# Routing of four mixture-of-experts stages: six slot one-hots on ScalarE, a residual shift moved behind the tiles, two of four weight guesses issued with the rows

## The chip, the cores and the metric

One core of one Trainium2 chip runs one program. The metric is the device time of one execution in microseconds, taken as the median over runs. Engines by their names in the profile: PE (TensorE), DVE (VectorE), ACT (ScalarE), POOL (GpSimd), SP (Sync, which here only issues DMAs); PEld is TensorE's weight load.

## The reference

Four layers over x of 1024 nodes x 256 features. Each layer adds a graph attention (or graph convolution) of the normalised x, and then a mixture of experts of the normalised x in which every row goes to its top two experts. The part that the change touches is the mixture, here that of layer 0, the residual form with a layer norm behind it:

```python
gate_logits = x @ gate_w + gate_b
topk_vals, topk_idx = jax.lax.top_k(gate_logits, K)            # K = 2
topk_w = jax.nn.softmax(topk_vals, axis=-1)
h = jax.nn.relu(jnp.einsum('bsh,ehf->bsef', x, w1) + b1)
expert_out = jnp.einsum('bsef,efh->bseh', h, w2) + b2
...
y = x + moe
return (y - mu) / jnp.sqrt(var + EPS) * gamma + beta
```

Layers 0 and 3 have 16 experts, layers 1 and 2 have 8; hidden widths are 512, 512, 1024 and 512 (layer 3 with two up projections and silu). Layer 2 adds one shared expert that every row passes through.

## The kernel before

The program runs four graph stages and four expert stages in turn, on all five engines, ordered by semaphores that are written out by hand; each engine executes its own queue in order. I call the expert stages 0 to 3 after their layers.

**Routing (`gate`).** An expert stage sorts its 2048 (row, expert) pairs into tiles of 128 rows of one expert. DVE makes one-hots of the chosen experts, TensorE counts ranks, and DVE derives for each pair a slot in its tile (`slot_f`, signalled by `slots_known`) and a tile (`on_tile`). The table of which row stands in which slot is a sum of 16 matmuls (`tensor_table`, L1490): the left factor is `on_slot`, 16 one-hots of 128x128, the right one `token`. Before the change GpSimd makes the first four `on_slot` one-hots (`pool_part`, L1509) and DVE the other twelve in one instruction (L1565); ScalarE makes one column of `token` (`scalar_column`, L1503, then a warm-up call of the stage's function, L1504). TensorE waits for all three, and then keeps itself busy with 56 matmuls of no result (`rouse`). `vector_rows` turns the sum into row numbers (`rows_known`, L1579), `first_rows` copies the first indices (L2008), and `vector_experts` writes the expert of each tile to `etab` (`tiles_known`, L1584).

**Expert tiles (`experts`).** Stages 0, 1 and 3 have UN = 4 buffers, stage 2 has 2. Per tile: GpSimd gathers 128 rows from DRAM with an indirect DMA (L1858, software queue q0), TensorE transposes them (`turn`, L1882), DVE copies them (L2004), TensorE multiplies by w1 (`rise`, L1894), ScalarE activates, and TensorE multiplies by w2 (`fall`, L1909) with operands that ScalarE and DVE split in two. Stage 2 first runs eight `own` tiles of the shared expert, with the routing between them.

**Weights (Sync queue, q1).** Before the routing is known, Sync loads a guessed expert into each of the UN buffers: two DMAs per buffer (L1810, L1811), about 1.05 MB together in stages 0 and 1, 1.57 MB in stage 3. Then it issues the load of the second biases (`biases.load`) and `after.prefetch`: in stage 0 five loads for the next graph stage, among them `gamma` and `beta`. Then it waits for `tiles_known`, and per tile reads the true expert and issues the DMA under the condition that the expert is another than the one guessed or held (L1829, L1834). A skipped DMA still counts up its semaphore, which `rise` waits for. In the timeline a skipped one of these shows about 0.01 to 0.1 us, an issued one 0.3 and more.

**The end of stage 0 (`BeforeGraph1`).** Its second half also works out the layer norm of the mixture with gamma and beta. `vector_early` runs on DVE ahead of the first tile: it prepares `a_parted` and a column of V, waits for gamma and beta, and adds beta to all of x (L1047). After the tiles TensorE sums the second biases, DVE adds them (L1651), the sums are loaded and normalised; GpSimd's powers (L972, L976) give the reciprocal deviations.

Of the kernel before, what the change touches and what calls it, by code (L numbers as in the profile page):

```python
# [15 lines left out]
P = 128  # L16
N = 1024
NT = N // P
# [8 lines left out]
def build(nc, A, out):  # L27
# [19 lines left out]
    with top:  # L47
# [27 lines left out]
        iota_p, spent = keep("iota_p", [P, 1]), keep("spent", [P, 1])  # L75
# [233 lines left out]
        class LastLayer:  # L309
# [25 lines left out]
            def vector_early(self, dve):  # L335
                pass
# [14 lines left out]
        class Handover:  # L351
# [3 lines left out]
            def vector_early(self, dve):  # L355
                pass
# [32 lines left out]
        def constants_vector(dve, link, iota_i, iota_pi, lane_i, turn_i, made, roused):  # L389
            nc.vector.memset(ones_b[:, :], 1.0).then_inc(roused, 1)  # L390
            nc.vector.memset(table[:, :], 0)
            nc.vector.memset(power[:, :, :], -0.5).then_inc(roused, 1)
            nc.vector.memset(xn[:, :, D:D + 1], 1.0)
            dve.wait_ge(made, 2)
            nc.vector.tensor_copy(iota_p[:, :], iota_pi[:, :])
            for un in (UN_NARROW, UN_WIDE):
                nc.vector.tensor_scalar(lane_i[un][:, :], iota_i[:, 0:32], un - 1, None, ALU.bitwise_and)
                nc.vector.tensor_scalar(turn_i[un][:, :], iota_i[:, 0:32], un.bit_length() - 1, None,
                                        ALU.logical_shift_right)
            link(nc.vector.tensor_copy(iota_row[:, :], iota_i[:, :]))  # L400
            nc.vector.tensor_scalar(code_row[:, :, :], bc(iota_row[:, 0:2 * NT].unsqueeze(2), [P, 2 * NT, 32]),
                                    float(CODE), None, ALU.add)
            link(nc.vector.tensor_scalar(own[:, :], iota_row[:, 0:32], float(P), float(OWN + CODE * P), ALU.mult, ALU.add))
            nc.vector.tensor_scalar(own[:, :], own[:, :], iota_p[:, :], None, ALU.add)
            for un in (UN_NARROW, UN_WIDE):
                nc.vector.tensor_copy(lane_rows[un][:, :], lane_i[un][:, :])
                nc.vector.tensor_copy(turn_rows[un][:, :], turn_i[un][:, :])
                nc.vector.tensor_scalar(part_rows[un][:, :], iota_row[:, 0:32], 1.0 / un, None, ALU.mult)
                nc.vector.tensor_scalar(iota_uns[un][:, :], iota_row[:, 0:32], float(un), None, ALU.mult)
# [515 lines left out]
        class BeforeGraph1(Handover):  # L925
# [4 lines left out]
            def __init__(self, ph):  # L930
                H, DH = self.H, self.DH
                self.rest = ph.sb("rest", [P, NT, H])
                self.dst = ph.sb("dst", [P, H, N])
                self.V = ph.sb("V", [P, NT, H, DH + 1])
                self.w = ph.sb("w", [P, DC, D])
                self.wr = ph.sb("wr", [P, DC, D])
                self.a = ph.sb("a", [P, DC, 2])
                self.a_parted, self.parted = ph.sb("a_parted", [P, DC, 2, 2]), ph.sem("parted")
                self.wa = ph.sb("wa", [P, DC, H])
                self.wab = ph.sb("wab", [P, DC, H, P])  # L940
                self.weights_loaded, self.post_loaded = ph.sem("weights_loaded"), ph.sem("post_loaded")
                self.folded, self.spread = ph.sem("folded"), ph.sem("spread")
                self.columns, self.valued = ph.sem("columns"), ph.sem("valued")
                self.columns_kept, self.values_kept = ph.sem("columns_kept"), ph.sem("values_kept")
# [23 lines left out]
            def gpsimd(self, pool):  # L968
                for t in range(NT + 1):
                    if t < NT:  # L970
                        pool.wait_ge(self.p_var_ready, t + 1)
                        nc.gpsimd.tensor_tensor(self.p_rstd[:, t:t + 1], self.p_moments[:, t, 1:2], power[:, t, :], ALU.pow)\  # L972
                            .then_inc(self.p_rstd_ready, 1)
                    if t >= 1:
                        pool.wait_ge(self.norm.var_ready, t)
                        nc.gpsimd.tensor_tensor(rstd[:, t - 1, :], mean_var[:, t - 1, 1:2], power[:, t - 1, :], ALU.pow)\  # L976
                            .then_inc(self.norm.rstd_ready, 1)
# [59 lines left out]
            def vector_early(self, dve):  # L1037
# [4 lines left out]
                for k in range(2):  # L1042
                    part = slice(k * DH, (k + 1) * DH)
                    self.link(nc.vector.tensor_copy(self.a_parted[part, :, k, :], self.a[part, :, :]))
                nc.vector.memset(self.V[:, :, :, DH:DH + 1], 1.0)
                dve.wait_ge(self.post_loaded, 32)
                self.link(nc.vector.tensor_tensor(x[:, :, :], x[:, :, :], bc(self.beta[:, :].unsqueeze(1), [P, NT, D]), ALU.add))  # L1047

            def vector(self, dve):
                H, link = self.H, self.link  # L1050
                nc.vector.memset(self.wa[:, :, :], 0.0).then_inc(self.parted, 1)
# [13 lines left out]
                def raised(t):  # L1065
# [3 lines left out]
                    dve.wait_ge(self.p_rstd_ready, t + 1)  # L1069
                    nc.vector.scalar_tensor_tensor(out=x[:, t, :], in0=z, scalar=self.p_rstd[:, t:t + 1], in1=x[:, t, :],  # L1070
# [366 lines left out]
        def gate(ph, L, E, all_probs, un, function, spare, room, dense):  # L1437
# [15 lines left out]
            POOL_SLOTS = 4  # L1453
# [18 lines left out]
            slots_known, on_slots = ph.sem("slots_known"), ph.sem("on_slots")  # L1472
# [27 lines left out]

            def scalar_column(act):
# [3 lines left out]

            def pool_part(pool):
                pool.wait_ge(slots_known, 1)
                for q in range(POOL_SLOTS):
                    ins = nc.gpsimd.tensor_scalar(on_slot[:, q, :], iota_row[:, :], slot_f[:, q:q + 1], None, ALU.is_equal)  # L1509
                ins.then_inc(on_slots, 1)  # L1510
# [48 lines left out]
            def vector_columns(dve):  # L1559
# [5 lines left out]
                nc.vector.tensor_tensor(on_slot[:, POOL_SLOTS:, :], bc(iota_row[:, :].unsqueeze(1), [P, 2 * NT - POOL_SLOTS, P]),  # L1565
                                        bc(slot_f[:, POOL_SLOTS:].unsqueeze(2), [P, 2 * NT - POOL_SLOTS, P]), ALU.is_equal)\
# [19 lines left out]
            def vector_dest(dve):  # L1586
# [13 lines left out]
                if dense:  # L1600
# [6 lines left out]
            return ((tensor_ranks, tensor_table), (scalar_exps, scalar_column),  # L1607
                    (vector_onehots, vector_slots, vector_tiles, vector_columns, vector_rows, vector_experts, vector_dest),
                    pool_part, tiles_known, rows_known, turns_known)
# [121 lines left out]
        def experts(L, E, F, kind, all_probs, own_loaded, w1_name, w2_name, b2_name, after):  # L1731
# [8 lines left out]
            with Phase(f"r{L}") as pr, Phase(f"e{L}") as ph:  # L1740
# [5 lines left out]
                gate_tensor, gate_scalar, gate_vector, gate_pool, tiles_known, rows_known, turns_known = \  # L1746
# [57 lines left out]
                def _(sp):  # L1804
# [4 lines left out]
                    for b in range(UN):  # L1809
                        sp.dma_start(w1[b][:, :], w1_v[guess(b), :, :]).then_inc(w1_loaded[b], 16)  # L1810
# [32 lines left out]
                def _(pool):  # L1843
# [22 lines left out]
                    gate_pool(pool)  # L1866
# [89 lines left out]
                def _(act):  # L1956
# [25 lines left out]
                    exps, column = gate_scalar  # L1982
                    exps(act)
                    if own:
                        own.round_weights(act)
                        for k in range(NT):
                            own.activate(act, k)
                            if k == 2:
                                column(act)
                    else:  # L1990
                        column(act)
# [6 lines left out]
                def _(dve):  # L1998
# [66 lines left out]
                    after.vector_early(dve)  # L2065
# [6 lines left out]
                    end(last, UN - 1)  # L2072
                    if biases:
# [90 lines left out]
```

## Time and profile before

| what | value |
|---|---|
| median of the runs | 1120.32 us (1111.72, 1120.32, 1123.72) |
| profiled execution | 1122.78 us, span 1121.0 us |
| mean granted TensorE clock | 0.906 of full speed |
| PE busy | 970.4 us (87%) |
| DVE / ACT / POOL busy | 711.5 / 503.8 / 472.6 us |
| DMA, queue q1 (Sync's) / q0 (GpSimd's) | 106.45 MB / 24.65 MB |

The span runs from the first to the last instruction of the profiled execution. The clock is the share of the full 2.4 GHz that was granted; at its lower level it is 0.5 (1.2 GHz). A row of the timeline gives the start, the length, the engine, the line, the operation, what it writes and reads, how many instructions are merged, and in brackets the idle time of the engine just before and what ended it. A time in the text without a unit is microseconds from the start of the span.

### The profile page before, as it was taken

The page shows a single profiled execution, that of the slowest core. Times are in us where ns is not written, and L with a number is a line of the kernel's source. Part 1 is how long each engine was busy: PE and PEld are TensorE (multiplying, and loading weights), DVE is VectorE, ACT ScalarE, POOL GpSimd, SP SyncE. Part 2 cuts the span into 40 slices and gives each one's busy share as a digit, 9 for nine tenths or more (in the row PEclk, how much of TensorE's full clock was granted, in tenths as well). Part 3 has the DMA queues.
Part 4 walks back from the last instruction along what each step waited for, and adds up shares of the span by engine and source line. Part 5 has one row for each costly group of instructions (what it writes and reads, how often), then busy time and mean ns, then how long its engine had stood idle before and what let it go on. Part 6 is the DMA issues. An engine that isn't in the chain of part 4 may idle for free. (4 is left out here: it accounts for less than half of the span.)

```text
span 1121.0 us, 22737 instructions
## 1 busy us (share of the span) xinstructions
PE 970.4 (87%) x7554; PEld 912.0 (81%) x7554; DVE 711.5 (63%) x1646; ACT 503.8 (45%) x965; POOL 472.6 (42%) x478
## 2 busy tenths in 40 slices
PE   6884999886899669969989999999899994999992
PEld 5584999685888669947989999999767883999992
DVE  4786677757777557768445366666566865566664
ACT  1341777035545447713015557777425431344431
POOL 1243676227776347610212045553234523345441
PEclk8696999898868979969998999999889996999997
DMA  6007864200000046543214001139400007645944
GB/s 245 2 29 261 289 223 154 90 1 1 11 11 11 28 166 227 178 133 126 82 62 169 11 25 38 42 117 335 165 5 1 15 15 270 243 155 172 323 160 132
DMA packets 57675, 132.30 MB, mean 118 GB/s; under 512 B 9664, under 2 KB 35712, under 8 KB 52864
## 3 DMA queue, kind: packets, MB, share of 16 engines
q1 hardware_dynamic: 47376, 106.45, 26.9%
q0 software_dynamic: 9024, 24.65, 7.2%
q8 instruction: 43, 0.70, 0.3%
q10 hardware_dynamic: 1200, 0.23, 0.1%
q14 instruction: 32, 0.26, 0.1%
HBM read 191.97 MB, written 17.56 MB: 187 GB/s over the span
## 5 line engine op out<-in xcount | busy, mean ns | idle before, releaser
L1894 PE MATMUL r_pH<-e_xsT,e_w 128*128 128x128 f32 x2304 | 280.9, 280 | 10.4 <-DVE e_xsT L2004 9.2
L1894 PEld LDWEIGHTS r_pH<-e_xsT,e_w 128*128 128x128 f32 x2304 | 271.8, 196 | 12.7 <-issue 12.4
L1848 POOL DMA_INDIRECT y_rows<-e_ys,e_to x94 | 157.9, 1680 | 185.3 <-DVE e_ys L2034 90.2
L1858 POOL DMA_INDIRECT e_xs<-xn_rows,e_idx x94 | 104.0, 1107 | 106.0 <-DVE e_idx L2008 81.0
L2020 DVE TENSOR_TENSOR e_w_lo<-e_w,e_w_hi 128x1024 fp32r<-128x1024 f32 (+1 forms) x94 | 137.9, 1467 | 11.6 <-ACT e_w_hi L1965 10.4
L1909 PE MATMUL r_pY<-e_w_hi,e_h_hi 128*128 128x256 f32 x464 | 138.8, 299 | 2.2 <-issue 2.2
L1965 ACT ACTIVATE e_w_hi<-e_w 128x1024 fp32r<-128x1024 f32 (+1 forms) x94 | 116.9, 1244 | 32.7 <-DMA e_w<-w_in 24.6
L1909 PE MATMUL r_pY<-e_w_lo,e_h_hi 128*128 128x256 f32 x464 | 131.1, 283 | 0.0
L1909 PE MATMUL r_pY<-e_w_hi,e_h_lo 128*128 128x256 f32 x464 | 131.0, 282 | 0.0
L501 ACT ACTIVATE g_t<-g_g,g_small 128x1024 f32<-128x1024 f32 x56 | 64.2, 1150 | 110.7 <-POOL g_small L488 110.7
L1909 PEld LDWEIGHTS r_pY<-e_w_hi,e_h_hi 128*128 128x128 f32 x464 | 88.6, 191 | 3.0 <-issue 2.9
L540 PE MATMUL g_tp<-ident,g_lm 128*128 128x128 f32 x448 | 68.5, 303 | 23.7 <-DVE g_lm L454 22.8
L1909 PEld LDWEIGHTS r_pY<-e_w_lo,e_h_hi 128*128 128x128 f32 x464 | 88.9, 192 | 0.0
L1909 PEld LDWEIGHTS r_pY<-e_w_hi,e_h_lo 128*128 128x128 f32 x464 | 88.6, 191 | 0.0
L2025 DVE TENSOR_TENSOR e_h_lo<-xnT,e_h_hi 128x512 fp32r<-128x512 f32 x72 | 49.8, 692 | 56.4 <-ACT e_h_hi L1981 47.7
L179 POOL TENSOR_SCALAR mean_var<-mean_var 128x1 f32<-128x1 f32 x36 | 25.8, 717 | 138.4 <-DVE mean_var L175 138.4
L454 DVE SCALAR_TENSOR_TENSOR g_lm<-g_g,g_small,g_t 128x1024 f32<-128x1024 f32 x56 | 71.7, 1281 | 17.3 <-ACT g_t L501 14.8
L540 PEld LDWEIGHTS g_tp<-ident,g_lm 128*128 128x128 f32 x448 | 57.9, 158 | 30.4 <-DVE g_lm L454 27.6
L551 PE MATMUL g_o<-n_V,g_pT 128*128 128x65 f32 x512 | 71.7, 301 | 4.0 <-ACT g_pT L510 4.0
L551 PEld LDWEIGHTS g_o<-n_V,g_pT 128*128 128x128 f32 x512 | 70.9, 221 | 4.9 <-ACT g_pT L510 4.9
L1977 ACT ACTIVATE xnT<-r_pH,e_w 128x128 f32<-128x128 f32 x176 | 50.2, 368 | 44.8 <-PE r_pH L1894 40.7
L446 DVE CUSTOM_DVE_ANT_0 g_g<-n_dst,neg 128x1024 f32<-128x1024 f32 x48 | 58.2, 1219 | 14.0 <-PEq L2084 14.0
(315 smaller groups left out, 1878.8 us busy)
## 6 DMA issues: line engine op xcount, KB each, us to landing
e_w<-w_in SPq DMA_DIRECT2D x56, 1024.0 KB
e_w<-w_in SPq DMA_DIRECT2D x84, 512.0 KB
e_w<-w_in SPq DMA_DIRECT2D x52, 514.0 KB
e_w<-w_in SPq DMA_DIRECT2D x24, 1028.0 KB
e_w<-y_rows SPq DMA_DIRECT2D x32, 256.0 KB, 4.9
p_adj<-adj_in SPq DMA_DIRECT2D x8, 512.0 KB, 10.4
xn_rows<-xn SPq DMA_DIRECT2D x32, 128.0 KB, 1.7
g_adjT<-adjT_in SPq DMA_DIRECT2D x8, 512.0 KB, 4.2
```

The costliest lines, as they stand in the source:

```text
L446: nc.vector.tensor_tensor_reduce(out=g[u % 4][:, :], in0=rows(u), in1=neg[:, u // heads, :], scale=1.0, scalar=-3e38, op0=ALU.add, op1=ALU ...
L454: nc.vector.scalar_tensor_tensor(out=lm[u % 2][:, :], in0=g[u % 4][:, :], scalar=b1[:, u:u + 1], in1=t2[u % 4][:, :], op0=ALU.add, op1=ALU ...
L501: nc.scalar.activation(t2[u % 4][:, :], g[u % 4][:, :], ACT.Identity, bias=b2[:, u:u + 1], scale=slope).then_inc(sloped, 1)
L540: ins = nc.tensor.transpose(tp[u % deep][:, c, :], lm[u % 2][:, c * P:(c + 1) * P], ident[:, :])
L551: ins = nc.tensor.matmul(o[k % 2][:, part, 0:width], pT[u % 2][:, c, :], values(u, c), start=(c == 0), stop=(c == NT - 1))
L1848: pool.indirect_dma_start(out=y_rows[:, :], in_=ys[b][:, :], in_offset=None, out_offset=bass.IndirectOffsetOnAxis(ap=to[b][:, :], axis=0))\
L1858: pool.indirect_dma_start(out=xs[b][:, :], out_offset=None, in_=xn_rows[:, :], in_offset=bass.IndirectOffsetOnAxis(ap=idx[b][:, :], axis=0))\
L1894: ins = nc.tensor.matmul(pH[b % 2][:, f, :], w1[b][:, at:at + P], xsT[b % 2][:, c, :], start=(c == 0), stop=(c == DC - 1))
L1909: ins = nc.tensor.matmul(pY[m][:, :], h[m][:, f, :], w[m][:, f * D:(f + 1) * D], start=(f == 0 and n == 0), stop=(f == FC - 1 and n == 2))
L1965: nc.scalar.activation(w2_hi[b % 2][:, :], w2[b][:, :], ACT.Copy).then_inc(w2_rounded, 1)
L1977: ins = nc.scalar.activation(hT[b % 2][:, f, :], pH[b % 2][:, f, :], function, bias=b1)
L2020: nc.vector.tensor_tensor(w2_lo[b % 2][:, :], w2[b][:, :], w2_hi[b % 2][:, :].bitcast(F32), ALU.subtract).then_inc(w2_split, 1)
```

## The change

- Routing: GpSimd makes no one-hots any more. ScalarE makes six: an Abs of (slot number minus column number) for each, 128x128, then one Relu of (1 minus that) over 128x768, which is 1 where the two are equal and 0 elsewhere. It does so ahead of its column of `token`; in stage 2 behind its second own tile. DVE makes ten instead of twelve.
- End of stage 0: the addition of beta to x moves from DVE ahead of the first tile to GpSimd behind its last store, and DVE's first `x` update waits for it (`shifted`). The other preparations of `vector_early` move behind the last tile, ahead of the second biases (`vector_idle`).
- Weights: Sync waits for `rows_known` before it loads the guesses of the third and fourth buffers. All that stands behind them on the Sync queue waits too. Stage 2, with two buffers, has no such wait.

```diff
@@ BeforeGraph1.gpsimd (the stage behind expert stage 0)
+                pool.wait_ge(self.post_loaded, 32)
+                nc.gpsimd.tensor_tensor(x[:, :, :], x[:, :, :], bc(self.beta[:, :].unsqueeze(1), [P, NT, D]), ALU.add)\
+                    .then_inc(self.shifted, 1)
                 for t in range(NT + 1):
...
-            def vector_early(self, dve):
+            def vector_idle(self, dve):
...
                     part = slice(k * DH, (k + 1) * DH)
-                    self.link(nc.vector.tensor_copy(self.a_parted[part, :, k, :], self.a[part, :, :]))
+                    ins = nc.vector.tensor_copy(self.a_parted[part, :, k, :], self.a[part, :, :])
+                ins.then_inc(self.parted, 1)
                 nc.vector.memset(self.V[:, :, :, DH:DH + 1], 1.0)
-                dve.wait_ge(self.post_loaded, 32)
-                self.link(nc.vector.tensor_tensor(x[:, :, :], x[:, :, :], bc(self.beta[:, :].unsqueeze(1), [P, NT, D]), ALU.add))
...
-                nc.vector.memset(self.wa[:, :, :], 0.0).then_inc(self.parted, 1)
+                link(nc.vector.memset(self.wa[:, :, :], 0.0))
...
                     dve.wait_ge(self.p_rstd_ready, t + 1)
+                    if t == 0:
+                        dve.wait_ge(self.shifted, 1)
...
@@ gate
-            POOL_SLOTS = 4
+            ACT_SLOTS = 6
+            apart = ph.sb("apart", [P, ACT_SLOTS, P], BF16)
...
+            def scalar_slots(act):
+
+                act.wait_ge(slots_known, 1)
+                for q in range(ACT_SLOTS):
+                    ins = nc.scalar.activation(apart[:, q, :], iota_row[:, :], ACT.Abs, bias=slot_f[:, q:q + 1], scale=-1.0)
+                ins.then_inc(measured, 1)
+                act.wait_ge(measured, 1)
+                nc.scalar.activation(on_slot[:, 0:ACT_SLOTS, :], apart[:, :, :], ACT.Relu, bias=one[:, :], scale=-1.0)\
+                    .then_inc(on_slots, 1)
...
-            def pool_part(pool):
-                pool.wait_ge(slots_known, 1)
-                for q in range(POOL_SLOTS):
-                    ins = nc.gpsimd.tensor_scalar(on_slot[:, q, :], iota_row[:, :], slot_f[:, q:q + 1], None, ALU.is_equal)
-                ins.then_inc(on_slots, 1)
...
@@ experts, Sync queue
                     for b in range(UN):
+                        if b == 2:
+                            sp.wait_ge(rows_known, 1)
                         sp.dma_start(w1[b][:, :], w1_v[guess(b), :, :]).then_inc(w1_loaded[b], 16)
...
@@ experts, GpSimd queue
-                    gate_pool(pool)
                     last = loop(pool, step)
@@ experts, ScalarE
                             own.activate(act, k)
+                            if k == 1:
+                                slots(act)
                             if k == 2:
                                 column(act)
                     else:
+                        slots(act)
                         column(act)
@@ experts, DVE
-                    after.vector_early(dve)
                     last = loop(dve, step)
...
                     end(last, UN - 1)
+                    after.vector_idle(dve)
                     if biases:
                         biases.add(dve, after.base)
```

## Rows read from the trace of the kernel before

**Rows 1.** The chain of waits, start of expert stage 3: start us, us, what

```profile
941.05 1.03 PE r_pH L1490 x16
...
942.62 0.19 DVE table L1579
...
943.82 6.28 DMA e_xs<-xn_rows,e_idx
...
950.15 0.45 PE r_pT L1882 x2
...
951.19 6.76 PE r_pH L1894 x32
```

**Rows 2.** Timeline, stage 3: start, us, engine line op out<-in [idle before <-releaser]

```profile
936.03 4.87 POOL L1509 TENSOR_SCALAR r_on_slot<-iota_row,r_slot_f 128x128 bf16<-128x128 f32 x4 [9.30 <-DVE r_slot_f L1549]
...
937.70 1.75 DVE L1565 TENSOR_TENSOR r_on_slot<-iota_row,r_slot_f 128x1536 bf16<-128x1536 f32 x1
```

**Rows 3.** Groups by line, ScalarE: busy us, mean ns, idle before

```profile
L1504 ACT ACT_TABLE_LOAD x2 | 2.6, 1283 | 0.0
...
L1503 ACT ACTIVATE r_token<-r_on_tile,iota_p 128x512 bf16<-128x512 bf16 x2 | 1.4, 721 | 9.2 <-DVE r_on_tile L1561 9.2
```

**Rows 4.** Timeline of ScalarE in stage 2

```profile
607.36 2.17 ACT L1706 ACTIVATE e_hT<-r_pH,own_own_room 128x128 f32<-128x128 f32 x8 [7.35 <-PE r_pH L1674]
```

**Rows 5.** Timeline, start of stage 0 (SPq: the Sync queue)

```profile
91.34 0.64 SPq L1810 DMA_DIRECT2D e_w<-w_in  x1
...
96.70 1.23 SPq L963 DMA_DIRECT2D e_beta<-L_ffn_beta_in  x1
...
99.25 1.01 PE L1490 MATMUL r_pH<-r_token,r_on_slot 128*128 128x64 bf16 x16 [8.22 <-POOL r_on_slot L1509]
...
101.99 0.17 DVE L1584 TENSOR_SCALAR etab<-r_et 1x32 int32<-1x32 f32 x1
...
104.22 0.01 SPq L1829 DMA_DIRECT2D e_w<-w_in  x1
...
106.25 2.29 DVE L1047 TENSOR_TENSOR x<-x,e_beta 128x2048 f32<-128x2048 f32 x1
...
106.46 0.44 PE L1882 MATMUL r_pT<-ident,e_xs 128*128 128x128 f32 x2 [1.20 <-DMA e_xs<-xn_rows,e_idx]
...
108.58 0.34 SPq L1829 DMA_DIRECT2D e_w<-w_in  x1
...
110.06 3.75 PE L1894 MATMUL r_pH<-e_xsT,e_w 128*128 128x128 f32 x16 [3.16 <-DVE e_xsT L2004]
```

**Rows 6.** DMA queues, 943.5 to 947.5: packets, MB, share of 16 engines

```profile
q1 hardware_dynamic: 310, 1.66, 101.2%
```

**Rows 7.** DMA queues, 947.5 to 950.5

```profile
q0 software_dynamic: 176, 0.50, 54.0%
q1 hardware_dynamic: 55, 0.18, 14.9%
```

**Rows 8.** Timeline, start of stage 1

```profile
393.53 4.34 POOL L1509 TENSOR_SCALAR r_on_slot<-iota_row,r_slot_f 128x128 bf16<-128x128 f32 x4 [7.57 <-DVE r_slot_f L1549]
...
398.01 0.80 PE L1490 MATMUL r_pH<-r_token,r_on_slot 128*128 128x48 bf16 x16 [7.31 <-POOL r_on_slot L1509]
...
400.54 1.12 POOL L1858 DMA_INDIRECT e_xs<-xn_rows,e_idx  x1 [2.68 <-DVE e_idx L2008]
...
405.01 0.44 PE L1882 MATMUL r_pT<-ident,e_xs 128*128 128x128 f32 x2 [1.96 <-DMA e_xs<-xn_rows,e_idx]
...
407.12 3.09 PE L1894 MATMUL r_pH<-e_xsT,e_w 128*128 128x128 f32 x16 [1.67 <-DVE e_xsT L2004]
```

**Rows 9.** Timeline of GpSimd, end of stage 0

```profile
200.57 0.97 POOL L1848 DMA_INDIRECT y_rows<-e_ys,e_to  x1 [1.49 <-DVE e_ys L2034]
...
211.30 0.74 POOL L972 TENSOR_TENSOR e_p_rstd<-e_p_moments,power 128x1 f32<-128x1 f32 x1 [9.76 <-DVE e_p_moments L1062]
```

**Rows 10.** One line's instructions: L1509, ns min/median/max, first and last start

```profile
L1509 POOL TENSOR_SCALAR r_on_slot<-iota_row,r_slot_f x16: 593/1007/3637, 94.2 to 939.9; 128x128 bf16<-128x128 f32 x16
```

## What the change will do to the time, predicted before it was run

> **What bounds the kernel now.** I read the page first: TensorE is busy 87% of the span, so the kernel runs at TensorE's pace except where TensorE stands still. The change touches only the start of the four expert stages and the end of the first, so I then read the chain of waits at the start of stage 3 [rows 1]. What to see: the 16 table matmuls wait for GpSimd's one-hots, three DVE steps follow, then the first row gather takes 6.28 us, and the first 32 matmuls take 6.76 us at the lower TensorE clock. Next the timeline of the same start [rows 2] and of stages 0 and 1 [rows 5, 8]: who else stands at the table, what the Sync queue issues when, and what delays the first tile. Last, the DMA queues' own shares in short stretches [rows 6, 7]: which queue moves bytes while the gather waits. That view decides the forecast.
>
> **The table (all stages).** Before, GpSimd starts its four one-hots at 936.03 and needs 4.87 us, to 940.90, and the matmuls start at 941.05; DVE's twelve are done at 937.70 + 1.75 = 939.45 [rows 1, 2]. After, ScalarE does six. Its 128x128 activations with a bias ran eight in 2.17 us [rows 4], mean step about 0.26, so six take 5 x 0.26 + 0.38 = 1.7. The Relu over 128x768 is not in the trace; 128x512 with a pointer operand takes 0.72 [rows 3], so it lies between 0.72 and 1.08; I take 1.0, near the 1.5-fold. The weighted column (0.72) now stands behind both. Sum: 936.03 + 1.7 + 0.1 + 1.0 + 0.7 = 939.5, matmuls at 939.6. DVE's ten end at 937.70 + 1.75 x 10/12 = 939.2, so ScalarE is the later. Gain 1.45 us (1.1 to 1.8) in stages 3 and 0, whose GpSimd block is the same; in stage 1, 393.53 + 3.6 against 398.01 [rows 8] gives 0.9. In stage 2 ScalarE stands idle 7.35 us before its third own tile [rows 4], which hides the 3.5 us; TensorE works on own tiles there: 0. GpSimd's four instructions go; it had nothing else to do before its gathers.
>
> **The late guesses (stages 0, 1, 3).** The wait sits on the Sync queue ahead of four weight DMAs and, in stage 0, ahead of the bias load and five prefetches. The rows are known 1.0 us before the first gather is issued (942.62 + 0.19 against 943.82 [rows 1]), and Sync needs no descriptors from GpSimd, so all four weight DMAs are issued before or while the gather's descriptors are made. What does the gather do behind queued weights? In stage 3 it is issued at 943.82; from 943.5 to 947.5 the software queue moved nothing and the weights' queue 1.66 MB in 4 us, 415 GB/s [rows 6]; only after that did the software queue run [rows 7]. It landed at 950.10, 2.2 us after the weights had drained near 947.9. In stage 1, where the weights were nearly through, gather to landing was 400.54 to 405.01, 4.47 us [rows 8]. So the gather is served behind whatever weights are ahead. Before, those were the rest of a burst begun early; after, a fresh burst starts just ahead of it, and between the two bursts the DMA engines stand idle.
>
> Stage 3: rows known at 942.8 - 1.45 = 941.4. From issue to first byte I take 0.8 us (bounds 0 and 1.5, the rows don't isolate it). 3.15 MB / 0.415 = 7.6 us, drained at 949.8, gather landed 2.2 later at 952.0, against 950.10: 1.9 later (bounds 1.0 and 2.6).
> Stage 1: rows known at about 399.5 - 0.9 = 398.6, plus 0.8, plus 2.1 MB / 0.415 = 5.1, plus 2.2: 406.7 against 405.01. Before, 1.7 us passed from the transpose's end (405.45) to the first block at 407.12, more than the 0.6 of stage 3, so part of the delay may vanish there: 1.2 later (0.5 to 1.7).
> Stage 0: here DVE's addition of beta, 2.29 us from 106.25, stood between the transpose at 106.46 and the first block at 110.06 [rows 5]; it is gone. The table is known at 99.6; the gather lands at 99.6 + 0.8 + 5.1 + 2.2 = 107.7, the block could start 1.05 later (950.15 to 951.19, as in rows 1) at 108.8. But Sync now issues the four weight DMAs and the six small ones after 99.6: before, that ran from 91.34 to 97.93, 6.6 us, so 106.2. Its first test, which the block waits for through the skipped load's semaphore, came 2.06 us after the expert table (101.99 + 0.17 to 104.22), so 108.3. Both give about 109.0 with slack: 1.1 earlier. The same 4 us on Sync moves the reload of buffer 2 from 108.58 to 112.6; its 0.5 MB lands near 116, when the third tile wants it: 0.2 back. Net 0.9 earlier (0.3 to 1.6).
> In stage 0 the guess of buffer 2 was wrong: a full DMA is issued at 108.58 [rows 5]. Delaying such a guess costs nothing by itself, and a right one is wanted only two tiles after the first; what costs is the burst ahead of the gather.
>
> **The clock.** TensorE stands idle longer ahead of the first block in stages 1 and 3 (matmuls end 1 to 1.5 us earlier, the gather lands later), so the blocks run wholly at 1.2 GHz. 16 matmuls of the first block took 3.75 in stage 0 and 3.09 in stage 1 [rows 5, 8], so up to 0.7 per block; I take 0.3 each, 0.6 (0 to 1.4).
>
> **The addition on GpSimd and the setup on DVE.** GpSimd's last store of stage 0 ends at 200.57 + 0.97 = 201.54, and it is next wanted for a power at 211.30, after 9.76 idle [rows 9]. No row has a 2048-element addition there. Bounds: DVE's 2.29 [rows 5], and 16 times the mean of the 128-element one-hots, 16 x 1.22 = 19.5; the undisturbed 0.593 [rows 10] x 16 is 9.5 and ends at 211.04. The mean was taken with DVE active beside it, and part of each is a start cost, so I take under 9.5: hidden, 0. The Trainium skill (GPSIMD Engine Reference, section 3.1, Elementwise) gives 4.5 us for just this shape, and 2.29 for VectorE, where the trace agrees with 2.29; by it the addition ends at 206.0 and the sum stays the same. The DVE setup (memsets and two small copies, 0.6 us) falls before the biases are added, where DVE waits for TensorE; if not covered it costs 0.6.
>
> **Sum.** -0.9 (stage 0) + 1.2 (stage 1) + 0 + 1.9 (stage 3) + 0.6 (clock) = +2.8 us. The profiled execution took 1122.78 (span 1121.0), which gives 1125.6; it lies 2.5 above the median of the runs shown, 1120.32, so I forecast 1123.1.
>
> **Rivals.**
> Even sharing between the queues. If the gather takes turns with the weights, it lands 4.5 us after issue: stage 3 at 946.8 instead of 950.1, 3.3 earlier, and TensorE's clock may still be at 2.4 GHz, so the 6.76 us block takes half, 3.4; stage 1 gains 0.9; stage 0 is held by Sync at 108.4, 1.65. Together 9.2 faster: 1111. For it: buffers 0 and 1 alone are queued early. Against it: the software queue's empty stretch [rows 6]. The Trainium skill (DMA: Bandwidth & Descriptors, Queues, rings and completion order) says each DMA engine goes round-robin over the queues that have work; that rule would give this rival, and rows 6 speak against it. Chance 0.17.
> GpSimd's addition is long. At 19.5 us it ends at 221.0, and the first power of the stage waits 9.7 us for it: with the forecast's 2.8, 1133. It decides from 9.8 us on. Against it: nothing disturbs it early. Chance 0.07.
> Table loads. If Abs or Relu needs another function table than Exp, a 1.28 us load [rows 3] stands in three stages: up to 3.8 more, 1127. For it: Abs occurs nowhere before. Against it: of the four warm-up calls behind the column only two needed a load [rows 3], and Relu's in stage 0 was not one of them. Chance 0.06.
> No net effect: the table's gain and the gather's delay cancel, 1120. Chance 0.15. The forecast itself: 0.55.
>
> **Numbers.** One per cent is 11.2 us, about what can be told from no change here: the three runs alone spread over 12 us. The range holds the forecast, the loads and the cancelling case, and reaches into even sharing: 1112 to 1128. Faster by over 1% needs all of even sharing and more, 0.06; slower by over 1% needs the long addition, 0.07; within 1%, 0.87.
>
> **What would show it.** Right: in stage 3 the table matmuls start about 3.5 us after the slots are known (5.0 before); the DMA engines show a gap before them; the software queue is again empty until the new weights have drained, and the gather takes about 9.5 us from issue. In stage 0 the first block starts near 109. Wrong: a gather of under 6 us while weights are in flight; a table load among ScalarE's one-hots; the first power of stage 0's end waiting for GpSimd's own addition.

## The result, and the profile after

| | before | after |
|---|---|---|
| median of the runs | 1116.50 us (1107.56 to 1123.72, 20 runs) | 1122.12 us (1115.14 to 1126.69, 20 runs) |
| profiled execution | 1122.78 us, span 1121.0 | 1123.03 us, span 1121.0 |
| mean granted TensorE clock | 0.906 | 0.905 |

The ratio of the times is 1.0049, with a 95% interval of 1.0034 to 1.0065: the changed kernel is 3.8 to 7.3 us slower. The forecast was 1123.1 us, +2.8 against the kernel before. The sign and the range held, and the size was half of what was measured. That 1123.1 lies within 1 us of the measured 1122.12 is luck: the base of the forecast, 1120.32, was 3.8 us above the median of the twenty runs, and the size was 2.8 us too small.

The two profiled executions have the same span. That of before stands near the slow end of its 20 runs (1122.78 against a median of 1116.50), and that of after 0.9 above its median. So the pair of traces shows where work moved, but the difference of medians can't be read from it. The kernels with one part of the change, below, are needed for that.

The timeline of after, start of stage 3 (start us, us, engine line op; in brackets the idle time before and what ended it). It answers to [rows 1, 2]:

```profile
936.42 1.86 ACT L1512 ACTIVATE r_apart<-iota_row,r_slot_f 128x128 bf16<-128x128 f32 x6 [3.24 <-DVE r_slot_f L1560]
938.32 0.94 ACT L1515 ACTIVATE r_on_slot<-r_apart,one 128x768 bf16<-128x768 bf16 x1
939.16 0.71 ACT L1520 ACTIVATE r_token<-r_on_tile,iota_p 128x512 bf16<-128x512 bf16 x1
...
939.96 1.01 PE L1497 MATMUL r_pH<-r_token,r_on_slot 128*128 128x64 bf16 x16 [6.67 <-ACT r_token L1520]
...
941.75 0.33 SPq L1823 DMA_DIRECT2D e_w<-w_in  x1
...
943.07 0.72 SPq L1824 DMA_DIRECT2D e_w<-w_in  x1
...
950.83 0.69 PE L1894 MATMUL r_pT<-ident,e_xs 128*128 128x128 f32 x2 [4.83 <-DMA e_xs<-xn_rows,e_idx]
```

ScalarE starts six one-hots at 936.42, and the table matmuls start 3.54 us later; before it was 5.0 from GpSimd's start. Sync's late guesses go out from 941.75 on. The chain of waits at the same place:

```profile
941.75 0.21 DVE e_idx L2023 x2
...
942.74 8.05 DMA e_xs<-xn_rows,e_idx
950.83 0.70 PE r_pT L1894 x2
951.55 0.44 DVE e_xsT L2019
...
952.13 5.22 PE r_pH L1906 x32
```

The gather takes 8.05 us where it took 6.28 [rows 1]: it is issued 1.55 us earlier in its stage and lands no earlier. The DMA queues of after (packets, MB, share of 16 engines), first 943 to 947, then 947 to 951, show why; they answer to [rows 6, 7]:

```profile
q1 hardware_dynamic: 247, 1.44, 87.4%
...
q1 hardware_dynamic: 121, 0.79, 51.7%
q0 software_dynamic: 78, 0.25, 47.4%
```

Until 947 the gather's queue moves nothing while the weights move 1.44 MB, as before the change. From 947 on both move. Of the 3.15 MB of late guesses 1.53 MB had moved by 947 and 2.27 MB by 950.8, where the gather landed. So the gather gets a share while 1.6 MB of weights is still on its way, and it is not last in a strict line. The gap ahead of the late burst is there too: the weights' queue was at 10% from 941.0 to 941.5. The Trainium skill (DMA: Bandwidth & Descriptors, Queues, rings and completion order) says the DMA engines take turns between queues that have work. The second stretch agrees with that. The first does not, if the gather's descriptors were ready, which no view shows directly. With nothing else in flight the gather's queue moved its first bytes 1.5 to 2 us after the issue (`gather_first`, below), and here it took 4.3.

The start of stages 0 and 1 of after, which answer to [rows 5, 8]:

```profile
98.75 1.26 POOL L1871 DMA_INDIRECT e_xs<-xn_rows,e_idx  x1 [16.30 <-issue]
...
102.23 0.47 SPq L965 DMA_DIRECT2D e_beta<-L_ffn_beta_in  x1
...
104.60 0.10 SPq L1842 DMA_DIRECT2D e_w<-w_in  x1
...
106.13 0.69 PE L1894 MATMUL r_pT<-ident,e_xs 128*128 128x128 f32 x2 [5.54 <-DMA e_xs<-xn_rows,e_idx]
...
107.42 3.75 PE L1906 MATMUL r_pH<-e_xsT,e_w 128*128 128x128 f32 x16 [0.61 <-DVE e_xsT L2019]
...
400.27 1.10 POOL L1871 DMA_INDIRECT e_xs<-xn_rows,e_idx  x1 [13.71 <-DVE e_idx L2023]
...
407.81 0.69 PE L1894 MATMUL r_pT<-ident,e_xs 128*128 128x128 f32 x2 [4.37 <-DMA e_xs<-xn_rows,e_idx]
```

In both, TensorE waits for the gather alone: 7.38 us from issue to transposes in stage 0, 7.54 in stage 1 (4.47 before, [rows 8]). Sync's first test, at 104.60, is in time. The end of stage 0, in the timeline of after, answers to [rows 9]:

```profile
196.86 0.34 DVE L1049 COPY n_a_parted<-n_a 64x4 f32<-64x4 f32 x2
...
198.55 4.51 POOL L972 TENSOR_TENSOR x<-x,e_beta 128x2048 f32<-128x2048 f32 x1
...
208.10 0.74 POOL L977 TENSOR_TENSOR e_p_rstd<-e_p_moments,power 128x1 f32<-128x1 f32 x1 [5.04 <-DVE e_p_moments L1066]
```

GpSimd's addition takes 4.51 us and 5.04 us of idle time still follow it: it is hidden. The Trainium skill's 4.5 us (GPSIMD Engine Reference, section 3.1) agrees.

**A common start for the stages.** Stage starts differ by some microseconds between executions. So below, each landmark is the time since the first guessed weight DMA of its stage on the Sync queue in the same trace. These starts are 89.36, 389.48 and 931.15 in before, and 87.20, 390.33 and 931.62 in after. "First block" is the start of the first tile's w1 matmuls, in brackets their length.

| | stage 0: transposes, first block | stage 1 | stage 3 |
|---|---|---|---|
| before | 17.10, 20.70 (3.75) | 15.53, 17.64 (3.09) | 19.00, 20.04 (6.76) |
| after | 18.93, 20.22 (3.75) | 17.48, 18.77 (3.58) | 19.21, 20.51 (5.22) |

### The profile page after: what moved, and what is told of

It is laid out like the page before. It is cut to its first block and busy times, and to the rows that moved or that the text cites. A ratio compares the mean times of both kernels' runs of the same rounds, so it can differ in the third digit from the quotient of the medians.

```text
span 1121.0 us, 22750 instructions
## 1 busy us (share of the span) xinstructions
PE 972.5 (87%) x7554; PEld 912.1 (81%) x7554; DVE 707.4 (63%) x1646; ACT 514.8 (46%) x993; POOL 454.8 (41%) x463
## 5 line engine op out<-in xcount | busy, mean ns | idle before, releaser
L552 PE MATMUL g_o<-n_V,g_pT 128*128 128x65 f32 x512 | 74.1, 308 | 4.1 <-ACT g_pT L511 4.1
L552 PEld LDWEIGHTS g_o<-n_V,g_pT 128*128 128x128 f32 x512 | 73.3, 228 | 5.1 <-ACT g_pT L511 5.1
L511 ACT ACTIVATE g_pT<-g_tp 128x512 f32<-128x512 f32 x112 | 60.4, 593 | 15.2 <-PE g_tp L541 15.1
## 6 DMA issues: line engine op xcount, KB each, us to landing
p_adj<-adj_in SPq DMA_DIRECT2D x8, 512.0 KB, 10.6
```

Source lines behind the costliest of these rows:

```text
L511: nc.scalar.activation(pT[u % 2][:, q, :], tp[u % deep][:, q, :], ACT.Exp)\
L552: ins = nc.tensor.matmul(o[k % 2][:, part, 0:width], pT[u % 2][:, c, :], values(u, c), start=(c == 0), stop=(c == NT - 1))
```

## The experiments

All ratios are to the kernel before, run beside it on the same chip, with 95% intervals. The kernels were run in several groups on different chips, so they are compared by these ratios rather than by their medians.

### The change without the wait, and the wait without the change

`no_wait` is after without Sync's wait:

```diff
-                        if b == 2:
-                            sp.wait_ge(rows_known, 1)
```

> The changed kernel without Sync's wait: the guesses of buffers 3 and 4 are issued at once again; ScalarE's one-hots and the moved addition stay. Backlog theory (the late guesses put a fresh burst of weights ahead of the first gather): this is the harmful part, and without it the kernel is faster than before, by 3 to 5 us: about 3 in stage 0 (no addition ahead of the first tile), 0.9 in stage 1, and 0 to 0.5 in stage 3, where the gather waits for the weights to drain whenever it is issued. Rival, one-hots or the addition are what costs: this stays slower than before by 3 to 6 us.

`wait_only` is before with these two lines:

> The kernel before with only the wait on the Sync queue. Backlog theory: slower by 6 to 9 us: in stage 3 the weights drain at about 951.3 instead of 947.9 and the gather lands 3.4 later; stage 1 2.6 later; stage 0 up to 2 later, as part hides behind DVE's addition. Rival (the wait is harmless, as guesses that are wrong are wanted late): within 1 us of before.

| | ratio | stage 0: transposes, first block | stage 1 | stage 3 |
|---|---|---|---|---|
| no_wait | 0.9994 (0.9968 to 1.0020) | 17.22, 18.27 (3.47) | 14.78, 15.83 (2.02) | 18.23, 19.28 (5.44) |
| wait_only | 1.0109 (1.0069 to 1.0149) | 19.99, 28.17 | 18.53, 19.82 | 20.91, 22.20 |

Between no_wait and after the transposes come 1.7, 2.7 and 1.0 us later, 5.4 together, and the first blocks 1.95, 2.94 and 1.23, 6.1 together. Nothing else differs between these two kernels. The medians, 1117.47 and 1122.12, are 4.65 apart, and the ratios differ by 0.55%, 6.1 us. The gain of 3 to 5 us over before that was expected of no_wait does not show (the interval is -3.6 to +2.2 us); its rival, 3 to 6 us slower, lies outside the interval. So the wait is what makes the changed kernel slower, and it does so through the gather. The timeline of no_wait in stage 1, with the DMA queues from 395.5 to 400.3 behind it:

```profile
395.50 1.10 POOL L1869 DMA_INDIRECT e_xs<-xn_rows,e_idx  x1 [13.45 <-DVE e_idx L2021]
...
400.34 0.44 PE L1892 MATMUL r_pT<-ident,e_xs 128*128 128x128 f32 x2 [1.81 <-DMA e_xs<-xn_rows,e_idx]
...
q1 hardware_dynamic: 243, 0.81, 41.7%
q0 software_dynamic: 132, 0.39, 25.3%
```

and of after the queues in the 4.5 us behind the same issue, 400.3 to 404.8:

```profile
q1 hardware_dynamic: 386, 1.45, 96.4%
q0 software_dynamic: 1, 0.00, 0.3%
```

Same gather, same issue. With the weights nearly through it takes 4.84 us; behind a fresh burst it moves next to nothing for 4.5 us and takes 7.54.

wait_only is about 12 us slower than before (7.7 to 16.6), where 6 to 9 were expected. The trace of stage 0 names a reason that the expectation had not priced:

```profile
103.97 0.44 SPq L963 DMA_DIRECT2D e_beta<-L_ffn_beta_in  x1
...
107.98 0.69 PE L1884 MATMUL r_pT<-ident,e_xs 128*128 128x128 f32 x2 [4.13 <-DMA e_xs<-xn_rows,e_idx]
...
111.78 0.36 DVE L1044 COPY n_a_parted<-n_a 64x4 f32<-64x4 f32 x2 [9.16 <-DMA n_a<-L_gnn_aT_in]
...
112.34 2.29 DVE L1047 TENSOR_TENSOR x<-x,e_beta 128x2048 f32<-128x2048 f32 x1
115.59 0.42 DVE L2006 COPY e_xsT<-r_pT 128x256 f32<-128x256 f32 x1 [0.95 <-DVE x L1047]
```

The loads for the next graph stage now go out behind the late guesses. DVE's early work waits 9.16 us for one of them, `n_a`, until 111.78; `beta` lands at about 112.1 (issue plus 8.1 us), and the addition follows at 112.34. The first copy, whose input has been ready since 108.7, stands behind all of it. So the wait costs about 12 us where DVE's early work stands ahead of the first tile, and about 6 where it has been moved away: the three steps of the change are not additive.

### The one-hots alone, and the moved addition alone

`acts_only` is before with the routing part, `shift_only` before with the addition and the DVE setup moved:

```diff
-            def pool_part(pool):
+            def scalar_slots(act):
...
-            def vector_early(self, dve):
+            def vector_idle(self, dve):
```

> The kernel before with only ScalarE's six one-hots in place of GpSimd's four. The table is known 1.1 to 1.5 us earlier in stages 0, 1 and 3. Backlog theory: stage 1 gains 0.9, where the weights are nearly drained; stage 3 gains nothing, since its gather waits for the drain; stage 0 gains nothing, since DVE's addition still stands ahead of the first tile: 0.5 to 1.5 faster in all. Rival (all of the earlier table arrives): 3.8 faster. Rival (ScalarE is the harm): slower.

> The kernel before with only the addition of beta moved to GpSimd behind the tiles and the small preparations behind the last tile. The addition takes about 4.5 us on GpSimd and hides; the first block of stage 0 starts about 2.5 us earlier: 2 to 3 us faster. Rival (the first tile then waits for something else, the gather or Sync): 0 to 1 us.

| | ratio | stage 0: transposes, first block | stage 1 | stage 3 |
|---|---|---|---|---|
| acts_only | 0.9999 (0.9971 to 1.0026) | 17.18, 20.77 (3.65) | 14.98, 16.03 (3.40) | 18.29, 19.58 (5.40) |
| shift_only | 0.9976 (0.9950 to 1.0002) | 17.25, 18.30 (3.55) | 14.37, 15.42 (2.02) | 18.53, 19.58 (5.44) |

With the one-hots on ScalarE the first gather is issued 1.18, 1.12 and 1.56 us earlier than before, and the transposes do not come earlier than in shift_only, which has GpSimd's one-hots: 17.18 against 17.25, 14.98 against 14.37, 18.29 against 18.53. In stages 1 and 3 shift_only is the kernel before, instruction for instruction. The gather lands when the guessed weights let it. So no gain of the shorter table shows as long as four buffers are guessed; the interval of acts_only, -3.2 to +2.9 us, can't tell the expected 0.5 to 1.5 us from none. The moved addition does what was expected: the first block of stage 0 comes at 18.30 instead of 20.70, and the ratio gives 2.7 us, though its interval just touches zero.

### Where the wait stands: behind the gather, or ahead of one buffer only

`gather_first` waits for the first gather's landing instead of the rows, `wait_b3` delays only the fourth buffer:

```diff
-                        if b == 2:
-                            sp.wait_ge(rows_known, 1)
+                        if b == 2:
+                            sp.wait_ge(xs_loaded[0], 16)
...
-                        if b == 2:
+                        if b == 3:
```

> The changed kernel, but Sync waits for the first gather to have landed (instead of the rows being known) before it issues the guesses of buffers 3 and 4. Nothing is then in flight beside the first gather. Backlog theory: it lands about 4.5 us after issue in every stage (7.4, 7.5 and 8.1 in the changed kernel), so the first block starts 2.9, 3.0 and 3.5 us earlier, if Sync's skipped loads do not hold it: those come behind ten more issues in stage 0 (6 us) and may hold it there. 5 to 8 us faster than the changed kernel, 0 to 3 faster than before. Rival (the gather is slow for another reason, such as its own descriptors): landing stays at 7 to 8 us after issue and the time stays that of the changed kernel.

> The changed kernel with the wait ahead of the fourth buffer's guess only, so the late burst is half as large (1.05 or 1.57 MB). If the delay of the gather follows the bytes of the burst, about half of the wait's cost returns: gathers land 1 to 1.5 us earlier than in the changed kernel in stages 0 and 1; 2 to 4 us faster than the changed kernel. Rival (the cost is that of Sync's own queue, not of bytes): nearly nothing returns, under 1 us.

gather_first: 1.0080 (1.0048 to 1.0111), slower than the changed kernel, where 5 to 8 us of gain were expected. The gather is free now: 3.3 us from issue to transposes in stage 0 (11.57 to 14.84), 5.0 and 3.8 in the others. Its queue moves the first bytes between 1.5 and 2 us after the issue. But everything behind the wait on the Sync queue is late, and the first block waits for the test of its own weights:

```profile
103.86 0.44 PE L1894 MATMUL r_pT<-ident,e_xs 128*128 128x128 f32 x2 [0.20 <-issue]
...
109.62 0.45 SPq L965 DMA_DIRECT2D e_beta<-L_ffn_beta_in  x1
...
111.96 0.10 SPq L1842 DMA_DIRECT2D e_w<-w_in  x1
112.08 2.29 PE L1906 MATMUL r_pH<-e_xsT,e_w 128*128 128x128 f32 x9 [7.78 <-DMA e_w<-w_in]
```

The first block starts 0.12 us after that test, at 23.06, and at 19.10 and 18.73 in the other stages, each 0.13 after its test. The second tile's own load goes out late as well, at 113.47, and its block starts at 30.70 where after has 25.01.

wait_b3: 1.0012 (0.9983 to 1.0041), transposes at 17.46, 15.58 and 18.03. With half of the late burst the ratio gives back 0.37 of the wait's 0.55% (4 us, with an interval that holds anything from little to all), and the transposes 4.6 of the 5.4 us. That is the side of the bytes; were it Sync's own queue alone, nearly nothing would have come back.

### No third and fourth guess at all

`direct34` is after with only two guesses; the true experts of the third and fourth tiles are loaded at once, without a condition.

```diff
-                    for b in range(UN):
-                        if b == 2:
-                            sp.wait_ge(rows_known, 1)
+                    for b in range(min(UN, 2)):
...
+                        if early(i, b, UN) and b >= 2:
+                            sp.nop(nofuse=True).then_inc(w1_loaded[b], 16)
+                            sp.nop(nofuse=True).then_inc(w2_loaded[b], 16)
+                            other = {}
```

> The changed kernel without guesses for buffers 3 and 4: when the true experts are known, Sync loads those directly, in its order. The gathers have landed by then. Backlog theory: gathers land 4.5 us after issue, Sync is free of the late issues, and the first blocks start about 3 us earlier in each of three stages; the loads of the third and fourth tile must land before they are wanted, about 9 us after the first block's start. 8 to 11 us faster than the changed kernel, 3 to 6 faster than before. Rival (the loads then come too late for tiles 3 and 4): the gain is given back at the third tile's first block.

The median is 1113.88 us, ratio 0.9956 (0.9927 to 0.9985): faster than both kernels, by about 5 and 10 us, as expected. The rival, a loss at the third tile, is not seen: its first blocks start at 25.92, 25.35 and 27.56, where after has 28.53, 26.78 and 31.85. The transposes of the first tile come at 14.87, 14.82 and 14.92. But the first blocks come at 18.05, 16.50 and 17.62, later than transposes and copy need:

```profile
102.62 0.44 PE L1896 MATMUL r_pT<-ident,e_xs 128*128 128x128 f32 x2
...
103.38 0.95 POOL L1873 DMA_INDIRECT e_xs<-xn_rows,e_idx  x1 [0.30 <-issue]
...
105.23 0.42 DVE L2021 COPY e_xsT<-r_pT 128x256 f32<-128x256 f32 x1 [4.54 <-remote]
```

DVE's copy could start at 103.06 and starts at 105.23, with no DVE instruction in between. `direct_pool` is direct34 with GpSimd's four one-hots back in place of ScalarE's six, to price the shorter table where no burst hides it:

> The kernel without guesses for buffers 3 and 4 (direct34), with the one-hots back on GpSimd. The table is then 1.1 to 1.5 us later in stages 0, 1 and 3. If the one-hots on ScalarE gain nothing only because the gather waits behind weights, they gain here, where it doesn't: this kernel is 3 to 4 us slower than direct34 and the first blocks start 1.1 to 1.5 us later. Rival (something else sets the first block's start, whenever the table is known): within 1 us of direct34.

1116.02 us, 0.9969 (0.9951 to 0.9986). First blocks at 19.22, 17.59 and 19.21: 1.2, 1.1 and 1.6 later than direct34. The table's gain now reaches the first block in full. In the times it is 0.13%, 1.5 us, where 3 to 4 were expected, and it is not separated from zero (0.9956 against 0.9969 with these intervals).

### TensorE's clock at the first block

`long_rouse` is after with 160 matmuls of no result behind the table instead of 56, `direct_rouse` is direct34 with 90:

```diff
-                    rouse(spare, 56)
+                    rouse(spare, 160)
```

> The changed kernel with 160 instead of 56 matmuls of no result behind the table, so that TensorE is busy until the first gather has landed. If the clock is what the idle time costs, the first block of stages 0, 1 and 3 runs at 2.4 GHz: 2 us instead of 3.75 and 3.6, 3.6 instead of 5.2, in all 4 to 5 us faster than the changed kernel. Rival (clock unaffected by it): no difference. If the 160 matmuls outlast the gather, the first transpose is delayed by what they outlast.

> direct34 with 90 instead of 56 matmuls of no result behind the table: they end about 16.2 us after the stage's start, where the first block starts at 16.5 to 18.05. If idle time ahead of the first block costs it the high clock, the first block takes 2 instead of 3.75 us in stages 0 and 1 and 3.8 instead of 4.2 in stage 3: 3 to 4 us faster than direct34. Rival: the matmuls delay the transposes by about 1.3 us, and the first block by as much: no gain.

long_rouse: 1.0047 (1.0022 to 1.0072), the same as after. Its first block in stage 0 is short:

```profile
108.58 0.39 PE L1894 MATMUL r_pT<-ident,e_xs 128*128 128x128 f32 x2
...
109.57 2.02 PE L1906 MATMUL r_pH<-e_xsT,e_w 128*128 128x128 f32 x16 [0.61 <-DVE e_xsT L2019]
```

16 matmuls take 2.02 us here, at a granted clock of 1.00 (2.4 GHz); in after they took 3.75 at 0.50 (1.2 GHz), when TensorE had stood idle ahead of them: 1.7 us per block. But the dummies ended 21.17 after the stage's start, the transposes stood behind them, and the first block came at 21.99 instead of 20.22. The clock gave 1.7 and the queue took 1.8. direct_rouse: 0.9967 (0.9949 to 0.9986), against 0.9956 without; the dummies ended at 17.84, 16.83 and 17.92, not at the 16.2 that was expected, and the transposes came at 18.27, 16.66 and 17.76 instead of 14.9. The first blocks start at 19.56, 17.66 and 18.76, 1.1 to 1.5 us later than in direct34. Only the one of stage 1 is shorter for it (2.02 instead of 3.75); that of stage 0 still ran at a granted clock of 0.50 and took 3.75. No gain either.

### What holds VectorE's copy

`lone_gather` is direct34 in which GpSimd issues only the first gather ahead of the first tile's copy, `pair_gather` the first two:

```diff
                         if not early(i, b, UN):
                             pool.wait_ge(turned, t - UN + 1)
+                        elif b == 1:
+                            pool.wait_ge(xsT_ready, 1)
```

> direct34, but GpSimd issues the second gather only when DVE has copied the first transposed tile. In direct34 that copy comes 5.9 us after the first gather's issue, 1 to 2 us after the transposes. If GpSimd's further gathers hold DVE's copy back, it now comes within 0.1 us of the transposes' end, 4 to 5 us after the issue, and the first block earlier by 1 to 2 us. Rival (they have nothing to do with it): still 5.9 us.

> The kernel with neither third nor fourth weights guessed (direct loads), whose GpSimd issues only the first two gathers ahead of the first tile and the third and fourth after the first tile's copy; nothing else changes. Theory (GpSimd's later gather instructions hold VectorE's copy, and the second tile must keep its early gather): transposes as in the direct kernel (14.8 to 14.9 us after the stage's first guess), copy within 0.1 us of their end (15.3, 14.6 to 15.3, 15.3), first block at 15.9, 15.2, 15.9 instead of 18.05, 16.50, 17.62, second tile's block straight behind the first (its copy under 19), and a time 3 to 5 us below the direct kernel's: ratio to before 0.991 to 0.994. Rival A (two gathers are enough to hold the copy, or the hold has another cause): copy again 1 us or more after the transposes, ratio as the direct kernel's, 0.9956. Rival B (what is won ahead of the first block is lost at the third tile, whose gather is now issued about 16.5 us after the first guess instead of 15): third tile's transposes wait for the gather, ratio 0.996 to 1.000.

In both, the copy follows the transposes at once. The timeline of pair_gather, stage 0:

```profile
102.14 0.95 POOL L1875 DMA_INDIRECT e_xs<-xn_rows,e_idx  x1 [0.30 <-issue]
...
103.89 0.44 PE L1898 MATMUL r_pT<-ident,e_xs 128*128 128x128 f32 x2 [1.55 <-DMA e_xs<-xn_rows,e_idx]
...
104.36 0.43 DVE L2023 COPY e_xsT<-r_pT 128x256 f32<-128x256 f32 x1 [2.41 <-PE r_pT L1898]
...
104.93 2.02 PE L1910 MATMUL r_pH<-e_xsT,e_w 128*128 128x128 f32 x16 [0.61 <-DVE e_xsT L2023]
105.56 0.94 POOL L1875 DMA_INDIRECT e_xs<-xn_rows,e_idx  x1 [2.48 <-DVE e_idx L2027]
...
106.79 0.38 PE L1898 MATMUL r_pT<-ident,e_xs 128*128 128x128 f32 x2
...
112.24 0.69 PE L1898 MATMUL r_pT<-ident,e_xs 128*128 128x128 f32 x2 [5.07 <-DMA e_xs<-xn_rows,e_idx]
```

The first blocks start at 15.92, 14.61 and 16.07 (15.91, 15.16 and 15.94 in lone_gather), the earliest of all kernels. Yet pair_gather takes 1123.66 us, 1.0066 (1.0045 to 1.0087). The third tile's gather, issued at 105.56 behind the copy, meets the direct weight loads and its tile's transposes start 6.68 us later; TensorE stands idle, and the third block takes 3.62 us at the low clock. Rival B had the mechanism and had it too cheap (0.996 to 1.000). lone_gather (1135.59 us in one run) has the same loss one tile earlier. So in direct34 the early third and fourth gathers hold the first copy by 0.7 to 2.2 us, and without them more is lost behind it.

## Why the prediction came out as it did

- **The table.** Forecast: matmuls 3.5 us after the slots are known. Measured: 3.54 (1.86 for the six, 0.94 for the Relu, 0.71 for the column). No table load stands among the one-hots. From the first guess on, the matmuls start 1.56, 1.12 and 1.56 us earlier in stages 0, 1 and 3, where 1.45, 0.9 and 1.45 were forecast. Right, each term within 0.25 us.
- **The rule for the gather.** Forecast: empty until the new weights have drained, then 2.2 us. The first 4 us were empty, as said, of which 1.5 to 2 us pass without any weights too (gather_first); then the queues shared. From rows known to transposes the forecast had 8.1, 8.1 and 10.6 us for stages 0, 1 and 3; measured 8.8, 8.5 and 9.1. Right in kind at first and wrong in the tail; 0.4 to 0.7 short in two stages and 1.5 long in stage 3. The step that was off there is "3.15 MB / 0.415 = 7.6 us": it put the gather behind all of the burst. From issue to landing it named about 9.5 us and it was 8.05.
- **Stage 3**, +1.9 forecast: the first block came 0.5 later than in the trace of before, 1.2 later than in no_wait. Over-sized.
- **Stage 1**, +1.2 forecast: +1.1 against the trace of before (18.77 against 17.64), so by the two traces it is right. That is luck. But shift_only has the same code in this stage as before, and there the first block starts at 15.42 and takes 2.02, where the profiled execution of before had 17.64 and 3.09. Its copy had been held, from 405.45 to 406.55. I saw the 1.7 us from transposes to block [rows 8] and took them as belonging to the kernel. Against shift_only, after is 3.35 later. This is the mis-sized term that counts.
- **Stage 0**, -0.9 forecast: first block 0.5 earlier (20.22 against 20.70). The forecast had Sync's tests at 108.3 and the gather at about the same time; Sync took 7.3 us from its first late guess to the first test, not 8.7, and the gather alone decided. Split by the experiments: the moved addition gives 2.4 and the wait takes 1.95 back (20.22 against 18.27).
- **The clock**, +0.6 forecast at 0.3 per block. The price between the levels is 1.7 us per block of 16 (3.75 against 2.02). Against shift_only the first blocks of after are 0.2, 1.56 and -0.2 us longer. Stage 1 is the place: with 56 dummy matmuls, blocks that started between 14.61 and 15.83 ran in 2.02, and those that started from 16.03 on in 2.46 to 3.78. Start alone does not set the length (direct_pool's block at 17.59 took 2.46, at a granted clock of 0.79), but the late gather moved the block from the first group into the second. "Up to 0.7 per block" was read from a block of before that was in the second group already (3.09 us, at 0.62).
- **The additions**, 0 forecast: right, 4.51 us on GpSimd with 5.04 idle behind it, and DVE's setup at 196.75 to 197.38 ahead of the biases. The rival of the long addition was wrong, and so was that of table loads.
- **Even sharing**, the rival on the faster side: wrong where it mattered, since no byte of the gather moved in the first 4 us; in the tail of the burst it holds by busy share (51.7 and 47.4%). Its 1111 us also lay just outside the range of 1112 to 1128 that was said to reach into it.

**The sum again.** Between the two profiled executions the starts of the first blocks moved by -0.5, +1.1 and +0.5 us and their lengths by 0, +0.5 and -1.5: +0.1 in all, as their equal spans say. So the forecast's +2.8 fits neither this pair nor the 5.6 us between the medians, and that its sign and range held is in part luck. With shift_only as the base in stages 1 and 3 and before in stage 0: first blocks -0.5 + 3.35 + 0.9, block lengths 1.56 - 0.2, together +5.1 us. Measured are +3.8 to +7.3, and 5.6 between the medians. The base was chosen after the result, and each trace is one execution, so this agreement is worth a microsecond or two and no more.

So the base was off, more than the mechanism. The sum was made on one execution that later proved to be 6.3 us above the median of twenty. In stages 1 and 3, where their code is the same, that execution is slower than shift_only's by 2.2 + 1.1 and 0.5 + 1.3 us at the first blocks. The forecast added the change to stalls that shift_only's execution does not have, and the change partly filled them. That they are rare in other executions of before is argued from its median; no second trace of it shows it.

## What to carry to other kernels

A transfer that the kernel waits for should not be issued right behind a burst of transfers that are needed later; here that cost 1.0 to 2.7 us per stage. Delaying a speculative load until its answer is known moves it to exactly the moment when the answer's own transfers start. If the load can wait, drop the guess and issue the right one (direct34). And each engine's queue is an order: what stands behind a new wait, or behind filler work, is paid for first, so an earlier first tile is worth nothing if the next tile's transfer was pushed back for it.

## What the runs showed of the hardware

- A GpSimd gather issued right behind or among 2 to 3 MB of weights from Sync moved next to nothing for 4 to 4.5 us (943 to 947 and 400.3 to 404.8 of after), then shared the engines. With nothing else in flight its first bytes moved 1.5 to 2 us after the issue, and it took 3.3, 5.0 and 3.8 us from issue to the transposes (gather_first).
- DVE's copy of a PSUM tile (0.42 us) started 0.7 to 2.2 us after the end of its transposes in direct34 and 1.1 us after it in stage 1 of before, and 0.04 us after them where GpSimd had no gather left to issue. In these held cases it began 0.9 to 1.1 us after the last of the four gather instructions ended. In stages 0 and 1 of shift_only and in stage 0 of gather_first four gathers stood there too and it was not held, so what exactly starts and ends the hold stays open.
